# Corner rows of the attention product folded into the bias row, row statistics read back from HBM, and a new order of mask loads, bias rows and paired low-rank blocks

## What is computed

```python
mod = (silu(c) @ wmod).reshape(8, 6, 1, 1024)          # sa, ca, ga, sb, cb, gb
ga, gb = clamp(ga), clamp(gb)                          # sign * max(|.|, 0.25)
h = layernorm(x) * (1 + ca) + sa
attn = (w1.T @ w2.T) * sparse_mask                     # [s, t], a band: 70 columns to each side of a 128-block
x = x + ga * gelu(h @ attn + b2)
h = layernorm(x) * (1 + cb) + sb
p = h @ U1                                             # low-rank product
gate, up = split(p @ V1 + b1)
x = x + gb * (((silu(gate) * up) @ U2) @ V2 + ffn_b2)
```

## Time and profile before

| what | value |
|---|---|
| median of 3 runs | 1170.33 us (1170.17 to 1173.3) |
| the profiled execution's own time | 1172.08 us |
| its span in the profile | 1170.3 us |
| TensorE busy | 1142.7 us, 98% |
| VectorE, ScalarE, GpSimd busy | 588.5, 490.1, 390.5 us |
| share of TensorE in the chain that ended last | 88% |

### The profile page before, as it was taken

How to read it: one execution, slowest core, us unless ns; L and a number is a source line. 1 busy time by engine, 2 the same in 40 slices (tenths; PEclk the granted TensorE clock), 3 DMA queues, 4 the chain that set the end, 5 groups by cost and what they waited for, 6 DMA issues and landing times.

```text
span 1170.3 us, 15391 instructions
## 1 busy us (share of the span) xinstructions
PE 1142.7 (98%) x5883; PEld 946.7 (81%) x5883; DVE 588.5 (50%) x941; ACT 490.1 (42%) x789; POOL 390.5 (33%) x339
## 2 busy tenths in 40 slices
PE   5899999999999999999999999999999999999998
PEld 4668989987888788888888888888888888888886
DVE  3568777885663335444434444343443434344344
ACT  2137767777886544233224224223322432432331
POOL 1028998971113765302113031221302113021210
PEclk9899999999999999999999999999999999999999
DMA  9997888777536541501321040140123105013001
GB/s 359 394 348 261 305 328 323 252 259 251 220 140 219 164 164 73 180 1 72 97 84 73 20 160 1 73 155 26 72 66 115 56 16 180 1 73 109 35 1 72
DMA packets 57484, 169.59 MB, mean 145 GB/s; under 512 B 6208, under 2 KB 11072, under 8 KB 55360
## 3 DMA queue, kind: packets, MB, share of 16 engines
q1 hardware_dynamic: 57408, 168.57, 40.1%
HBM read 126.51 MB, written 42.04 MB: 144 GB/s over the span
## 4 chain that ended last, share of the span: by engine, by line
PE 88%; DMA 3%; SPq 2%; DVE 2%; POOL 2%; issue 1%; ACT 1%; DVEq 0%; POOLq 0%; ACTq 0%
PE bank L546 22%; PE bank L548 21%; PE bank L547 21%; PE bank L728 8%; PE bank L609 4%; PE bank L930 3%; PE bank L937 2%; PE bank L932 2%; PE bank L583 2%; DMA w2t_sb<-in_w2t 1%; PE bank L714 1%; POOL g L1603 1%; SPq L379 1%; POOL xs L1606 1%; PE bank L910 1%
## 5 line engine op out<-in xcount | busy, mean ns | idle before, releaser
L1169 ACT ACTIVATE act<-bank,b_sb 128x512 f32<-128x512 f32 (+1 forms) x176 | 121.3, 690 | 497.3 <-PE bank L548 481.4
L1518 DVE SCALAR_TENSOR_TENSOR act<-bank,b_sb,act 128x512 f32<-128x512 f32 (+1 forms) x176 | 132.0, 750 | 376.3 <-PE bank L548 353.2
L546 PE MATMUL bank<-pt,v_hi 128*128 128x512 f32 x688 | 268.6, 390 | 0.0
L547 PE MATMUL bank<-pt,v_hi 128*128 128x512 f32 x688 | 267.8, 389 | 0.0
L548 PE MATMUL bank<-pt,v_lo 128*128 128x512 f32 x688 | 267.6, 389 | 0.0
L1674 POOL TENSOR_TENSOR x2t<-gbb_bc,x2t 128x512 f32<-128x512 f32 x64 | 86.5, 1374 | 244.8 <-DMA x2t<-x_dram 244.8
L1528 DVE TENSOR_TENSOR act_lo<-act,act_hi 128x512 fp32r<-128x512 f32 (+1 forms) x176 | 160.4, 912 | 0.8
L546 PEld LDWEIGHTS bank<-pt,v_hi 128*128 128x128 f32 x688 | 129.1, 188 | 29.5 <-DVE act L1518 2.6
L548 PEld LDWEIGHTS bank<-pt,v_lo 128*128 128x128 f32 x688 | 129.2, 188 | 26.9
L547 PEld LDWEIGHTS bank<-pt,v_hi 128*128 128x128 f32 x688 | 129.2, 188 | 26.7
L546 PE MATMUL bank<-act_hi,u_hi 128*128 128x512 f32 x336 | 131.0, 390 | 0.7 <-DVE act_lo L1528 0.6
(11 more groups left out here) (134 smaller groups left out, 1663.3 us busy)
## 6 DMA issues: line engine op xcount, KB each, us to landing
xs<-in_x SPq DMA_DIRECT2D x32, 512.0 KB, 5.2
wm_sb<-in_wmod SPq DMA_DIRECT2D x8, 2048.0 KB, 10.8
x_dram<-xs SPq DMA_DIRECT2D x32, 512.0 KB, 5.3
xs<-x_dram SPq DMA_DIRECT2D x32, 512.0 KB, 5.9
x2t<-x_dram SPq DMA_DIRECT2D x32, 512.0 KB, 4.0
out<-x2t SPq DMA_DIRECT2D x31, 512.0 KB, 4.9
pt_dram<-pt_st SPq DMA_DIRECT2D x8, 1024.0 KB, 4.3
pt<-pt_dram SPq DMA_DIRECT2D x8, 1024.0 KB, 5.6
```

The lines of the kernel that those rows point to most:

```text
L546: nc.tensor.matmul(acc, s_hi, m_hi, start=start, stop=False)
L547: nc.tensor.matmul(acc, s_hi, m_lo, start=False, stop=False)
L1169: nc.scalar.activation(act[0:w, j % 2, :], bank[0:w, j % 2, :], ACT.Silu, bias=b1_sb[0:w, i, 0:1]).then_inc(silu_done, 1)
L1518: nc.vector.scalar_tensor_tensor(act[0:w, j % 2, :], up, b1_sb[0:w, i, 1:2], act[0:w, j % 2, :], ALU.add, ALU.mult).then_inc(act_done, 1)
```

## The change

1. Corner rows. `fold` holds, for each half, 96 rows of `attn_hi` of the block that only reaches over the border (70 columns of them) and 16 rows of bias (high and low), which `fold_turn` gathers with two small matmuls; no row of the 32 left out may have anything in the corner, which two more checks of the mask (`CORNERS`) make sure of. For b > 0, `y_end` uses `corner` (96 rows of `h_hi` and 32 rows of `pick`) as stationary and `fold` as moving operand, and `y_part` leaves out the hi x hi matmul of that block. ScalarE writes `corner`: `corner_pick` once and `corner_rows` once (half 0) or twice (half 1) for each batch and half.

```diff
-                nc.tensor.matmul(bank[:, n, :], pick[:, b:b + 1].to_broadcast([P, P]),
-                                 beta[:, h * HALF:(h + 1) * HALF], start=False, stop=True,
...
+                nc.tensor.matmul(bank[:, n, :], corner[:, h, toks], fold[:, h, :], start=False, stop=True,
...
+                terms = [(h_hi, attn_hi), (h_hi, attn_lo), (h_lo, attn_hi)]
+                if b > 0 and part == CORNERS[h][:3]:
+                    del terms[0]
...
+            def corner_rows(b, h):
+                i = b * FB + CORNERS[h][0]
+                ae.wait_ge(hi_ready, i + 1)
+                ae.wait_ge(y_done, (b - 1) * 8 + (h + 1) * TT)
+                for rows in ((slice(0, KEPT),), (slice(SPARE, 2 * SPARE), slice(2 * SPARE, P)))[h]:
+                    nc.scalar.activation(corner[rows, h, :], h_hi[rows, i % RING, :],
+                                         ACT.Copy).then_inc(corner_ready[h], 1)
...
+                hi(b, 5)
+                corner_rows(b, 0)
+                hi(b, 6)
...
                 split(0)
+                corner_pick(b, 1)
                 gelu(b, 1)
+                corner_rows(b, 1)
```

```diff
                 first_gates_turn(0)
+                beta_product(1, whole)
+                first_gates(0)
                 mod_product(5)
-                first_gates(0)
-                beta_product(1, whole)
+                y_near(0, 4)
                 mod_turn(5)
-                y(0, 4, whole)
+                y_end(0, 4, whole)
```

```diff
-                for k in range(4):
+                for k in (0, 2):
                     turn(t, 4 + k)
+                    turn(t, 5 + k)
                     p_product(b, k)
...
+                    p_product(b, k + 1)
```

The read-back now stands right behind the stores of the last batch, and the 16 small stores of gate rows stand behind the read-back of the batch after it. Besides, `raw_load(5)` goes ahead of the last `pt_store`, and in the feed-forward stage each `weight_hi` stands one block later:

```diff
-                    if at_start(b, EARLY + i - 1 < PIECES):
-                        weight_hi(EARLY + i - 1)
+                    if at_start(b, 1 < i < PIECES - EARLY + 2):
+                        weight_hi(EARLY + i - 2)
```

215 lines of the change are left out of this document (131 added, 84 removed).

## The result

| | median (us) | range | ratio to before, 95% interval |
|---|---|---|---|
| before | 1170.33 | 1169.28 to 1173.3 | |
| changed | 1181.13 | 1178.35 to 1183.29 | 1.0083 (1.0065 to 1.0101) |

The changed kernel is slower by 10.8 us, where 5.9 less was forecast.

A forecast was written before the change was run, and what follows sets the result against it. TensorE was taken as the bound, busy 1142.7 of 1170.3 us. Terms -6.2 - 0.3 + 2.6 + 2.25 - 3.6 - 0.6 = -5.85 took the median from 1170.33 to 1164.4, range 1161.5 to 1169.0.

The forecast's parts named there:

- 0 in a normal batch: Attention batches: ScalarE's five new copies, about 0.52 us each, fit its slack and cost TensorE nothing.
- Corners, -6.2: Attention batches: dropping 56 hi x hi matmuls of 70 columns at 0.111 us each saves 6.2 us; batches last 21.0.
- The rival of the cheap corner: Attention batches: weight loads are hidden, so the 56 corner matmuls save 0.9 us, not 6.2; total 1169.7, chance 0.03.
- Start, -0.3: Start: of a us or more won at TensorE's wait for w2t, only 0.3 us is left, behind load-bound wmod products.
- First batch, +2.6: First batch: VectorE waits 2.7 us for chunk 5, TensorE idles 2.0 before the bias; costs 2.6 us.
- The dip: Clock falls behind the new idles of the first or last attention batch, 1.6 us each; one 0.27, both 0.10.
- Last attention batch, +2.25: Last attention batch: three ScalarE copies delay the transposes by 1.9 us, VectorE's later splits add 0.35 at the second bias.
- The second dip that the rival named: Last attention batch: the clock also falls behind its idle of 1.9 us; both dips give 1167.6, chance 0.10.
- Low-rank product, -3.6: Low-rank product: the read-back queued earlier removes VectorE's wait, TensorE's 1.95 us idle and the slow clock's 1.7.
- 0 for the pairs: Low-rank product: paired transposes save or cost 0.087 us in each of 32 places, ±2.8; taken as 0.
- Feed-forward, -0.6: Feed-forward: weights loaded one place earlier and split one block later remove TensorE's 0.64 us idle at 385.45.
- The slower rival: Every batch: ScalarE's copies become the bound; at 1.3 us per copy the total is 1177; chance 0.06.

The follow-up runs named there:

- e11: Changed kernel with 32 small matmuls at the start and SP's old order at the low-rank product's start (weights and stores ahead of the read-back): 1174.93 us.
- e9: Changed kernel: VectorE's bias before chunk 5's copy, 32 small start matmuls, last batch's second-half corner rows behind last normalisation, `pick` copy one block later: 1165.03 us.
- e18: e9 with 6 small matmuls (24 instructions) at the start instead of 32: 1165.89 us, 0.9955 of the kernel before.
- e1: Changed kernel with TensorE's order in the first batch as before: 1176.12 us.
- e2: Changed kernel with VectorE's copy of chunk 5 moved behind the statistics, aggregate and low part of the bias's second half: 1176.63 us.
- e13: Kernel before the change with 38 small matmuls (152 instructions) added in TensorE's wait at the start: 1174.37 us, 1.0023 of the kernel before.
- e5: Changed kernel with 32 small matmuls (128 instructions) added in TensorE's wait at the start: 1173.25 us.
- e4: Changed kernel with 128 small matmuls (512 instructions) added in TensorE's wait at the start: 1183.19 us.
- e7: Changed kernel with single transposes in the low-rank product, as before, instead of pairs: 1184.48 us.
- e8: Changed kernel: e2's VectorE order, 32 small start matmuls, `pick` copy two blocks later, last batch's second U1 split and two corner copies behind last normalisation: 1168.5 us.

## Why the prediction was wrong

Three steps failed: the join of the branches stood in the sum at nothing and cost 6.7 us, the slow clock behind the idle in the first batch was priced at 1.6 us and cost 6.4, and "0 in a normal batch" for ScalarE's copies cost 3.6. By its own steps:

- **Corners, -6.2.** The mechanism and the size of one are right: a matmul of 70 columns is worth 0.11 us, and batch 1 took 20.97 us where 21.0 was forecast. The rival of the cheap corner is refuted. The sum over batches 1 to 6 was -1.7 instead of -5.3. The step that failed is "0 in a normal batch": it looked at the two places where ScalarE's rows are wanted, and not at VectorE behind ScalarE's `hi`, nor at batches 5 and 6, whose chunks are the gate's. They took 22.6 us and not 21.0, 1.6 more each.
- **Start, -0.3.** Measured -0.3.
- **First batch, +2.6.** The wait was forecast at 2.7 and measured at 2.76, the idle at 2.0 and 2.08. But the place cost +9.0. In five other executions batch 1 is only 3.7 to 4.1 us late, and of this about 1.7 is a short fall of the clock (0.57 over 4 us in e11), so the delay itself was sized rightly at 2.6. The dip was a rival with its price taken from one row, 1.6 us at 283, where TensorE had stood for 1.95. That was the wrong row to size it by: here the clock stayed at half for over 12 us, and TensorE's work in it took nearly twice as long. A dip has no fixed price: in those five executions the row's 1.6 would have been about right.
- **Last attention batch, +2.25.** With the corners' own 0.9 taken off, +1.4 was forecast and +1.3 measured: 2.08 us of idle against 1.9 (the three copies took 1.84 us of ScalarE and not 1.56), and nothing at the second bias against 0.35. The runs that moved the two copies (e9, e18) halved the wait. The second dip that the rival named, behind this idle, didn't come in the changed kernel's profile (clock 1.00 from 245 to 250), but did in e1's and e2's.
- **Low-rank product, -3.6 and 0 for the pairs.** Measured -4.9 from the stage's seventh product on. The wait and the slow clock went. But the cause was put down too surely to the queue's order, which is worth 1.6 us (e11). In the kernel before, the wait hangs on when TensorE comes to this place: in e13, which comes 6.2 us later by the stall, the idle is gone with the old order too, and the stretch is 3.8 us shorter. The pairs bring 0.8.
- **Feed-forward, -0.6.** Measured -1.0 there, from the last hi x hi product of U1 to the end.
- **Not in the sum: the join, +6.7.** The row "issue" of 1.2 us stood in the view of waits before, and I did not ask what it was. Nothing in the forecast priced the length of the program. It is the largest term that the sum didn't have: with 24 or 128 instructions more at the start, where TensorE waits anyway, the second stall is gone and the median 4.0 and 7.9 us lower (of e5's 7.9 the profile gives 5.6 to the join; its clock in the first batch was better too).

So the forecast lost 6.4 us by the clock, 6.7 by the join and 3.6 in batches 1 to 6, 16.7 together, and the low-rank product and what is behind it gave 1.7 more than was forecast, the last attention batch 0.1: 14.9, from 5.9 below to 9.0 above in the span. The slower rival was the wrong one: ScalarE's copies take 0.52 to 0.66 us from start to start, and did not bound every batch.

## What to carry to other kernels

Where an engine's order is changed on one side only (TensorE asks for the bias earlier, VectorE still makes it behind a chunk), price the new wait, and then the clock behind it with a range and not a number. Behind a join of branches, look for stalls that the profile calls issue and for the packets of the instruction queue next to them (and first for a wait in the program whose data came just then): a change that takes instructions out can put a join at a piece's end, and a few harmless instructions in an idle stretch move it away again. A small gain taken off the bound in every round is spent quickly by copies on an engine that another engine is waiting for; check the whole chain behind that engine, in the round with the most extra work.

## What the runs showed of the hardware that was not expected

- **Instruction fetch.** Behind the join TensorE stands 1.2 to 2.6 us, and a second time for 4.4 to 6.0 us where the piece fetched first holds only few instructions: 8 matmuls with their weight loads in the changed kernel, in e1 to e4 and in e7, 12 in e13. The first stall ends 2.5 to 2.8 us after a packet of the instruction queue begins (3.2 to 3.5 in e8, e9 and e18), the second 2.3 to 2.5, beside a read-back of 2 MB. Shifts by 256 and 512 instructions leave it in place, by 24, 112 and 128 take it away; 152 bring it into a kernel that had none, 40 don't.
- **The clock behind an idle.** After an idle of 2.08 us the granted clock was 0.50, which is 1.2 GHz, for 12 us in the changed kernel (91 to 103); in e11, with the same idle at the same place, it was 0.57 from 88 to 92 and 1.00 from 92 on; in e5, it was 1.00 from 80 to 100 us and fell only to 0.83 from 100 to 110, behind an idle of 1.46.
- **Small operations on VectorE beside GpSimd.** 128 x 32 values take 0.18 us while GpSimd stands (at 76.4 in the changed kernel), and up to 1.23 us when they start beside one of GpSimd's products of 128 x 512 (1.28 to 1.30): they end 0.04 us behind that product. An operation that starts in the gap between two products takes 0.18 again (at 206.78, where one ends at 206.83). The Trainium skill, page "SBUF — State Buffer", section "Who interferes with whom", says that VectorE and GpSimd share a pair of ports, and that of two operations which need it the one that starts first holds it for its whole length while the other stands; these ends agree with that.
